# Hybrid conv, attention and mixture-of-experts kernel: the first batches rebuilt, with constants in order of need, weights over two queues, expert weights split later and the slot fill in pieces

## What is computed

```python
# conv mixer
xn = (x - mean) / sqrt(var + 1e-5) * ln_w + ln_b          # over channels
bcdt = conv3x3(einsum('bchw,oc->bohw', xn, w_bcdt), w_gw, groups=32)
BC, dt = split(bcdt, 2)
AB = softmax(dt + A, over positions) * BC
y = einsum('bcs,bsn->bcn', einsum('bcn,bsn->bcs', x, AB), BC)
x = einsum('bchw,oc->bohw', y, w_out) + x
# attention over the 1024 tokens of a batch, u = _ln_t(t)
q, k, v = lrelu(u @ Wq + bq), lrelu(u @ Wk + bk), lrelu(u @ Wv + bv)
t = t + gamma * norm(softmax(mask(q @ k.T / 8)) @ v + u) + beta
# experts: one of 8 for each of 32768 tokens, capacity 5120 rows each
idx, prb = argmax and max of softmax(u2 @ gate_w + gate_b)
t = t + prb * (relu(u2 @ w1[idx] + b1[idx]) @ w2[idx] + b2[idx])   # where a row was free
```

## Time and profile before

| what | value |
|---|---|
| median of three runs | 2148.56 us (2146.14 to 2151.14) |
| the profiled execution | 2159.72 us |
| its span, first to last instruction | 2157.5 us |
| TensorE matmuls busy | 1991.0 us, 92% |
| VectorE busy | 1750.4 us, 81% |
| ScalarE busy | 1196.4 us, 55% |
| GpSimd busy | 1088.2 us, 50% |
| mean granted TensorE clock | 0.968 |

### The profile page before, as it was taken

The page is one execution under the profiler, slowest core; times in us unless marked ns, Lnnn a source line. Parts: engine busy times, 40 slices in busy tenths (PEclk is TensorE's granted clock), DMA queues, the critical chain, the costliest instruction groups (busy, mean ns, idle before and its releaser), DMA issues. The chain is left out here.

```text
span 2157.5 us, 41952 instructions
## 1 busy us (share of the span) xinstructions
PE 1991.0 (92%) x13855; PEld 1639.8 (76%) x13855; DVE 1750.4 (81%) x5467; ACT 1196.4 (55%) x2216; POOL 1088.2 (50%) x1243
## 2 busy tenths in 40 slices
PE   1669999999999999999999999999839999999996
PEld 1347787877878788787887878877629998888985
DVE  2257888888888888888888888888739998888985
ACT  0135555555555555555555555555427777777773
POOL 3111445555545545455454554544436665555554
PEclk9679999999999999999999999999959999999997
DMA  4911221221212212122121221212137777777874
GB/s 164 397 40 32 58 70 50 57 74 51 70 50 57 74 51 69 51 56 74 53 67 50 57 74 54 63 39 54 39 111 204 205 234 259 259 242 256 244 244 172
DMA packets 163511, 243.97 MB, mean 113 GB/s; under 512 B 31039, under 2 KB 110478, under 8 KB 163296
## 3 DMA queue, kind: packets, MB, share of 16 engines
q1 hardware_dynamic: 146016, 209.46, 32.2%
q0 software_dynamic: 17280, 31.84, 4.5%
HBM read 115.95 MB, written 95.56 MB: 98 GB/s over the span
## 5 line engine op out<-in xcount | busy, mean ns | idle before, releaser
L1184 PE MATMUL pvp<-va,pT 128*128 128x129 f32 x4096 | 503.3, 275 | 0.4 <-ACT pT L727 0.3
L1184 PEld LDWEIGHTS pvp<-va,pT 128*128 128x128 f32 x4096 | 484.1, 191 | 21.5 <-issue 11.1
L641 POOL DMA_INDIRECT expert_slots<-rows,slot_i x256 | 378.0, 1476 | 99.3 <-issue 89.8
L1355 POOL DMA_INDIRECT token_rows<-res x284 | 308.8, 1087 | 231.8 <-DVE res L1488 162.3
L727 ACT ACTIVATE pT<-stp 128x512 f32<-128x512 f32 x512 | 293.1, 596 | 132.9 <-PE stp L1158 126.9
L839 DVE TENSOR_REDUCE mxs<-mxp 128x1 f32<-128x512 f32 x512 | 336.0, 683 | 37.6 <-PE mxp L1061 27.3
L1541 PEld LDWEIGHTS e_yp<-w2s,hid 128*128 128x128 f32 x2272 | 294.2, 192 | 20.3 <-ACT hid L1418 0.3
L1541 PE MATMUL e_yp<-w2s,hid 128*128 128x128 f32 x2272 | 299.9, 275 | 0.0
L1418 ACT ACTIVATE hid<-e_hp,b1c 128x512 f32<-128x512 f32 x284 | 195.3, 688 | 113.8 <-PE e_hp L1533 105.5
L1061 PE MATMUL mxp<-khi,qhi 127*128 127x512 f32 x512 | 218.4, 469 | 13.7 <-issue 11.2
L1156 PE MATMUL stp<-qhl,klh 128*128 128x512 f32 x512 | 223.5, 436 | 3.1 <-DMA qhi<-nt 1.9
(11 more groups left out here) (242 smaller groups left out, 3836.6 us busy)
## 6 DMA issues: line engine op xcount, KB each, us to landing
w1p<-w_parts SPq DMA_DIRECT2D x71, 512.0 KB
expert_slots<-fill SPq DMA_DIRECT2D x32, 660.0 KB, 11.3
e_rows<-expert_slots SPq DMA_DIRECT2D x71, 264.0 KB, 4.9
w2s<-in_w SPq DMA_DIRECT2D x71, 256.0 KB
xs<-in_x SPq DMA_DIRECT2D x32, 512.0 KB, 4.8
token_rows<-rows SPq DMA_DIRECT2D x32, 512.0 KB, 3.8
f_rows<-token_rows SPq DMA_DIRECT2D x32, 512.0 KB, 6.9
out<-f_cols SPq DMA_DIRECT2D x32, 512.0 KB, 7.5
```

The lines of the kernel that those rows point to most:

```text
L641: g.indirect_dma_start(out=slots, out_offset=bass.IndirectOffsetOnAxis(ap=slot_i[k][:, t:t + 1], axis=0), in_=rows[k][:, t, :], in_offset= ...
L1184: last = mm(pvp[qt % 2][:, 0:VA], pT[c][:, kt, n * P:(n + 1) * P], va[k][:, kt, :], start=(kt == 0), stop=(kt == NT - 1))
L1355: g.indirect_dma_start(out=tokens, out_offset=bass.IndirectOffsetOnAxis(ap=res[n % 2][:, q, TOKEN:TOKEN + 1].bitcast(I32), axis=0), in_=re ...
```

## The change

The steps of a batch and their arithmetic stay. What changes:

- SP: x of batch 0, six loads on the new semaphore `w_first` (tap weights, w_bcdt_t, ln_w, w_bcdt_t again, ln_b, gate weights), x of batch 1, then w1 of experts 0 and 1. No further prologue.
- ScalarE's own queue: the other twelve loads (bq and bk on `bq_loaded`, ten on `w_loaded`).
- GpSimd: ident, mean_m (`ident_ready`); gmask, wtap, gwc, qkscale, img, neghalf (`early_ready`); pairs, the filler (`fill_ready`); the state selector after the root of batch 0's x statistics (`state_ready`); then all other constants (`mask_ready`).
- TensorE and VectorE: wln and the three small products come first and go to `mxp[0]`; the tap transposes (to `pvp`) come behind x_turn of batch 0, the tap copies behind its statistics. Waits for weights and constants stand at the first step that uses them.
- w1 of expert e is split on VectorE in step xs of batch 4 + e; SP stores it and loads w1 of expert e + 2 in step x_turn of batch 5 + e.
- The slot fill is issued from ScalarE's queue, two stores at a time, ahead of the steps bT_turn, dt, cd_turn, u1_turn, qk and qk_high until all 32 are out.
- `head`, `steps` and `tail` are written anew (484 steps in the head).

```diff
+FILL_STEP = 2
+W1_FIRST = 4
-        NW = 18
+        NW, NFIRST = 10, 6
@@ steps, one round of the loop
-        steps = [("t1b", 0), ("g", 2), (("mx", 0, 7), 1), (("st", 1, 7), 0), (("negmax", 0), 1), ("y", 2),
-                 (("mrow", 0), 1), ("ts", 2), (("pv", 1, 0), 0), ("u2_turn", -1), ("ln3s", -1), (("pv", 1, 1), 0),
-                 ("x_turn", 3), (("st", 0, 0), 1), ("xs", 3), (("u1n", 0), 2), (("u1n", 1), 2), (("pv", 1, 2), 0),
-                 ("gate", -1), (("pv", 1, 3), 0), (("u1n", 2), 2), (("st", 0, 1), 1), (("mx", 1, 0), 1),
...
+        steps = [(("mrow", 1), 0), ("t1b", 0), ("mask", 1), ("conv", 2), ("qk_high", 1), ("qk_low", 1),
+                 (("ln2n", 3), -1), ("dt", 2), ("dt_exp", 2), (("st", 1, 0), 0), (("st", 1, 1), 0), ("ln2m", -1),
...
+                 (("st", 1, 7), 0), ("y", 2), (("pv", 1, 0), 0), (("mrow", 0), 1), ("ts", 2), ("u2_turn", -1),
+                 (("pv", 1, 1), 0), ("gate", -1), ("ln3s", -1), (("pv", 1, 2), 0), (("u1n", 0), 2), (("u1n", 1), 2),
+                 (("u1n", 2), 2), (("mx", 1, 0), 1), (("pv", 1, 3), 0), (("st", 0, 0), 1), (("u1n", 3), 2),
+                 ("gate_turn", -1), (("st", 0, 1), 1), ("x_turn", 3), (("mx", 1, 1), 1), (("mx", 1, 2), 1),
...
@@ head, behind ts of batch 0
-                (0, "cd_turn"), (0, "h"), (0, "hh"), (0, "g"), (0, "y"), (0, "ts"), (0, ("u1n", 0)), (0, "mask"),
-                (0, ("u1n", 1)), (0, ("u1n", 2)), (0, ("u1n", 3)), (1, "x_turn"), (0, "u1_turn"), (1, "xs"),
-                (0, "qk"), (0, "v"), (1, "bcdt"), (1, "bT_turn"), (0, "t1b"), (0, "qk_lrelu"), (1, "conv"), (1, "dt"),
...
+                (0, "cd_turn"), (0, "h"), (0, "hh"), (0, "g"), (0, "y"), (0, "ts"), (1, "x_turn"), (0, ("u1n", 0)),
+                (0, ("u1n", 1)), (0, "mask"), (0, ("u1n", 2)), (0, ("u1n", 3)), (0, "u1_turn"), (1, "xs"), (0, "qk"),
+                (0, "qk_lrelu"), (0, "qk_high"), (0, "v"), (1, "bcdt"), (0, ("mx", 0, 0)), (0, ("mx", 0, 1)),
+                (0, "t1b"), (1, "bT_turn"), (0, ("mx", 0, 2)), (0, ("mx", 0, 3)), (0, "qk_low"), (0, ("mx", 0, 4)),
+                (1, "conv"), (1, "dt"), (1, "dt_exp"), (0, ("mx", 0, 5)), (0, ("mx", 0, 6)), (0, ("mx", 0, 7)),
+                (0, ("negmax", 0)), (0, ("mrow", 0)), (1, "cd_turn"), (0, ("mx", 1, 0)), (1, "h"), (0, ("st", 0, 0)),
...
@@ sync
-            w(wbc[:, 0, :], w_bcdt_t)
...
-            for e in range(E):
...
-            for f in range(NFILL):
...
+            sp.dma_start(gw_s[:], gate_w).then_inc(s["w_first"], 16)
             load_x(1, 1)
...
+            load_w1(0)
+            load_w1(1)
...
+                if st == "x_turn" and W1_FIRST < b <= W1_FIRST + E:
+                    e = b - W1_FIRST - 1
+                    wait_apart(sp, s["w1_parts"], e * 2 + 2, passed["sp"])
+                    sp.dma_start(w1parts[e], w1h[e % 2][:]).then_inc(w1_stored[e % 2], 16)
+                    if e + 2 < E:
+                        load_w1(e + 2)
@@ gpsimd
+            g.memset(neghalf[:], -0.5).then_inc(s["early_ready"], 1)
...
+                    if first:
+                        state_constants()
+                        pool.wait_ge(s["state_ready"], 1)
+                        late_constants()
@@ scalar
-            act.wait_ge(s["w_loaded"], 16 * NW)
-            act.wait_ge(s["mask_ready"], 1)
...
+            def fill_slots():
+                if filled[0] == 0:
+                    act.wait_ge(s["fill_ready"], 1)
...
+                for f in range(filled[0], min(filled[0] + FILL_STEP, NFILL)):
+                    act.dma_start(slots[f * P * FILL_ROWS:(f + 1) * P * FILL_ROWS].rearrange("(p r) d -> p (r d)", p=P),
+                                  fill[:].rearrange("p r d -> p (r d)")).then_inc(s["fill_done"], 16)
+                    filled[0] += 1
...
+                if st in ("bT_turn", "dt", "cd_turn", "u1_turn", "qk", "qk_high") and filled[0] < NFILL:
+                    fill_slots()
@@ vector
+                    if first:
+                        taps()
+                    if W1_FIRST <= b < W1_FIRST + E:
+                        w1_part(b - W1_FIRST)
@@ tensor
+            pe.wait_ge(s["w_first"], 16 * NFIRST)
+            pe.wait_ge(s["ident_ready"], 1)
             pe.wait_ge(s["wln_ready"], 1)
-            pe.wait_ge(s["taps_ready"], 1)
-            mm(work[:, 1, 256:256 + U], mean_m[:], wln[:], start=True, stop=True)
+            mm(mxp[0][:, 0:U], mean_m[:], wln[:], start=True, stop=True)
```

More of the change, by code:

```diff
@@ L530, in chain @@
                 pool.wait_ge(s["const_pool"], cp[0])
-            chain(g.memset(fill[:], 0.0))
-            g.memset(fill[:, :, TOKEN:TOKEN + 1].bitcast(I32), NO_TOKEN).then_inc(s["fill_ready"], 1)
             chain(g.memset(ident[:], 0.0))
@@ L536, in _ @@
                                   base=0, channel_multiplier=1))
-            chain(g.memset(ones_bf[:], 1.0))
-            chain(g.affine_select(out=before_bf[:], in_=ones_bf[:], pattern=[[1, P]], compare_op=ALU.is_gt, fill=0.0,
-                                  base=0, channel_multiplier=-1))
-            chain(g.tensor_copy(ident_bf[:], ident[:]))
-            chain(g.memset(mean_m[:], 1.0 / C))
-            chain(g.memset(pairs[:], 0.0))
-            for d in (U - S, U, U + S):
-                chain(g.affine_select(out=pairs[:], in_=pairs[:], pattern=[[-1, U]], compare_op=ALU.not_equal, fill=1.0,
-                                      base=-d, channel_multiplier=1))
-            chain(g.memset(wtap[:], 0.0))
-            chain(g.memset(ident2[:], 0.0))
-            for d in range(2):
-                for j in range(Q4):
-                    own = ident2[:, d * S:(d + 1) * S]
-                    chain(g.affine_select(out=own, in_=own, pattern=[[-1, S]], compare_op=ALU.not_equal, fill=1.0,
-                                          base=-j * S, channel_multiplier=1))
+            g.memset(mean_m[:], 1.0 / C).then_inc(s["ident_ready"], 1)
             gm = gmask[:].rearrange("o (g i) -> o g i", i=2)
@@ L583, in _ @@
             chain(g.memset(img[:], 0.0))
-            for k in range(2):
-                chain(g.memset(qhi[k][U:P, :].bitcast(F32), 0.0))
-                chain(g.memset(qhi[k][U:U + 1, :].bitcast(F32), 1.0))
-                chain(g.memset(khi[k][U:P, :].bitcast(F32), 1.0))
-                chain(g.memset(va[k][:, :, C:VA], 1.0))
-            g.memset(neghalf[:], -0.5).then_inc(s["mask_ready"], 1)
+            g.memset(neghalf[:], -0.5).then_inc(s["early_ready"], 1)
+            pool.wait_ge(s["early_ready"], 1)
@@ new lines, in _, with state_constants @@
+            chain(g.memset(pairs[:], 0.0))
+            for d in (U - S, U, U + S):
+                chain(g.affine_select(out=pairs[:], in_=pairs[:], pattern=[[-1, U]], compare_op=ALU.not_equal, fill=1.0,
+                                      base=-d, channel_multiplier=1))
+            chain(g.memset(fill[:], 0.0))
+            g.memset(fill[:, :, TOKEN:TOKEN + 1].bitcast(I32), NO_TOKEN).then_inc(s["fill_ready"], 1)
+            def state_constants():
+                chain(g.memset(ident2[:], 0.0))
+                for d in range(2):
+                    for j in range(Q4):
+                        own = ident2[:, d * S:(d + 1) * S]
+                        ins = g.affine_select(out=own, in_=own, pattern=[[-1, S]], compare_op=ALU.not_equal, fill=1.0,
+                                              base=-j * S, channel_multiplier=1)
+                        if (d, j) == (1, Q4 - 1):
+                            ins.then_inc(s["state_ready"], 1)
+                        else:
+                            chain(ins)
@@ L860, in one @@
                 if st == "dt":
+                    if first:
+                        dve.wait_ge(s["w_loaded"], 16 * NW)
                     dve.wait_ge(s["conv_done"], b + 1)
@@ L1092, in one @@
                 if st == "conv":
+                    if first:
+                        pe.wait_ge(s["taps_ready"], 1)
                     pe.wait_ge(s["img_ready"], b + 1)
@@ L1099, in one @@
                 if st == "cd_turn":
+                    if first:
+                        pe.wait_ge(s["state_ready"], 1)
                     wait_apart(pe, s["cd_exp"], b + 1, passed["pe"])
@@ L1116, in one @@
                 if st == "g":
+                    if first:
+                        pe.wait_ge(s["w_loaded"], 16 * NW)
                     pe.wait_ge(s["h_ready"], b + 1)
@@ L1136, in one @@
                 if st == "mask":
+                    if first:
+                        pe.wait_ge(s["mask_ready"], 1)
                     pe.wait_ge(s["kflag_ready"], b + 1)
```

190 lines of the change are left out of this document (102 added, 88 removed), and 332 rows, old and new, of tables (head, steps, tail).

## The result

| | before | after |
|---|---|---|
| median of 20 runs each | 2151.31 us | 2142.63 us (2139.3 to 2149.46) |
| ratio, 95% interval | | 0.9958 (0.9948 to 0.9968) |
| profiled execution, its span | 2159.72, 2157.5 us | 2142.42, 2140.7 us |
| TensorE busy | 1991.0 us | 2003.1 us |

Faster, by 0.42% or about 9 us (the 2148.56 us in the table of the kernel before is the median of three of these runs); I had forecast 47 and a range that ended at 2121.

A forecast was written before the change was run, and what follows sets the result against it. TensorE bounds the middle; the start is a chain through all engines. Head 52, less 1 for expert weights, 3 for the loop and 1 for the drain, gives 47 us: 2148.56 to 2101 us, range 2087 to 2121.

The forecast's parts named there:

- Constants, weights, taps: Start of the kernel: constants by need, two weight queues, taps apart; batch 0's statistics at 12.9 us, not 49.25: 36.3 us.
- New order of the head: Head up to batch 2's convolution: that starts at 109 us instead of 161.7, gain 52 us including the 36.3.
- Fill in pieces: Slot-fill stores on ScalarE's queue until batch 2: cost 0.3 us twice on the path, bounds 0 and 40 us.
- Rival 1: Head, batches 0 to 2: fill transfers delay q,k parts and score rows, giving back 20 us: 2121; chance 0.20.
- Expert weights in batches 4 to 11: Eight weight splits moved into these batches cost VectorE between 0 and 9 us; taken as 1.
- New order of the loop: Repeated steps: costs 0.1 us a batch, 3 us over 27 batches, between -4 and +14.
- Rival 3: Loop: TensorE stalls at gate behind u2's copy and at second-half maxima, 2 us a batch, 54 us: 2155; chance 0.05.
- The drain: End of the token part: eight score tiles stand together at ScalarE's pace, costing 1 us.
- rival 2: Head: TensorE's clock is full throughout, 9 us less, 1 already counted: 2093; chance 0.13.
- The test I had set: Batch 2's image at 108 us with a gain under 40 us blames the loop; its period says by how much.

The follow-up runs named there:

- prologue alone: Changed kernel with the head, steps and tail lists of the kernel before; constants, weights, split and fill as changed: 2124.15 us, 0.988 of the kernel before.
- order alone: Kernel before with only the three new lists (head, steps, tail): 2178.64 us, 1.0147 of the kernel before.
- fill in batch 0: Changed kernel with five fill stores a step instead of two during batch 0: 2139.29 us, 0.9948 of the kernel before.
- the new head and the old loop and drain: Changed kernel with the new head order cut to 513 steps, loop and tail of the kernel before: 2115.10 us, 0.9836 of the kernel before.
- gamma early: Changed kernel with loop steps ln2m and ln2g moved right behind the last ln2n, ahead of dt: 2207.96 us, 1.0271 of the kernel before.
- second try: Changed kernel with u2_turn and gate one pv later, second half's first maxima behind the second score tile: 2222.35 us, 1.032 of the kernel before.
- scatter right behind pos: Changed kernel with the loop's scatter step moved right behind pos, instead of behind the last maxima: 2255.71 us, 1.0497 of the kernel before.
- third try: Changed kernel with u2_turn and gate one pv later, second half's first maxima right behind the first score tile: 2138.95 us, 0.9944 of the kernel before.

## Why the prediction was wrong

**Constants, weights, taps: right.** First statistics 12.15 us (12.9 worked out), t1 38.29 (39.2), u1 44.37 (45.3). The gate weights were issued at 3.95 us and landed 2.8 us later, at 6.8, ahead of my 8.0. The prologue alone passed the 36.3 us on in full (36.6 at batch 1, 37.9 at batch 2) and then lost 7.1 between batches 2 and 3, in the same place as the changed kernel. Its fill pieces travel beside q,k parts there as well; no run took them away, so for that run the cause is argued.

**New order of the head: right to batch 2.** Maxima at 62.83 (64), conv of batch 1 at 66.51 (68.2), t1 at 84.53 (86.5), conv of batch 2 at 110.28 (109): 51.4 us against 52. Where I went wrong is that I ended the account at that convolution. 52 us was the lead there, and I took the lead there for the gain. The sum 52 - 1 - 3 - 1 = 47 has no term for the stretch from batch 2 to 3; as measured it is 51.5 - 12.4 - 24.5 - 4.5 = 10.1, with the expert weights inside the 24.5.

**Fill in pieces: the step that failed in the head.** I had 0.3 us twice and looked at what the stores cost ScalarE. Their price fell on SP's queue: a mask row behind q,k parts, 5.6 us of TensorE, with VectorE's queue behind it. Of the 12.4 us by batch 3, 8 go when that wait goes or falls to 1.6 us (46.9 and 47.0 us from batch 2 to 3 instead of 54.9). Some 4 stay, also in the order alone, which has no pieces on ScalarE's queue (46.5, against 42.5 before); what they are is open. Part of the 12.4 is the clock: TensorE's busy time in the stretch is 47.70 us at 0.91 here, 43.89 at 1.00 with the fill in batch 0 (42.46 before). Rival 1 named the mechanism, with 20 us for what cost 8. Its argument against fails twice. The pairs are not 5 us apart (109.69 and 111.25 us belong to two). And a small row needs more than an engine's time: 2.19 us of issue and 8.3 us until its reader starts, while the engines' share is 1.00.

**Rule and row.** The DMA share of 1.00 from 110 to 120 us, with stores from one queue and q,k parts from another, is where the rule cited in the prediction (the Trainium skill, DMA: Bandwidth & Descriptors, "Issuing engines are not separate DMA queues") bears: transfers interleave on the same 16 engines whoever starts them. I used it for the weights, where it changed nothing, and not for the fill, where it spoke against a free move. The trace agrees with it there.

**Expert weights in batches 4 to 11: right.** The period is 45.89 us in batches 7 to 11 and 45.77 later, 0.12 us for each split, 1 us in all (I took 1).

**New order of the loop: the term that was mis-sized, and the sign of the surprise.** I took 0.1 us a batch with an upper end of 14 us; it was 0.89, 24.5 us to batch 31, beyond that end. The 0.1 had no row behind it; in its place stands the wait behind GpSimd, 0.53 us a batch, and 0.36 that stay open. "No row prices this" was wrong: the trace had the slack, though not in the rows I showed. Before, beta ended 3.4 us ahead of t1, and reading the wait ahead of L896 and what stands on GpSimd in front of it would have shown a chain one could check against the new lists. Rival 3 had the sign, the wrong place (gate and u2's copy) and a price twice too high; 24.5 us was not enough to turn the sign.

**The drain: mis-sized too.** I took 1 us. From the image of batch 31 to the expert part's first matmul it is 139.2 us before, 143.7 in the changed kernel, 139.6 in the prologue alone and 139.7 with the new head and the old loop and drain. The runs with the new last steps have 142.2 to 144.0, with two buffers for t1 or three. So the 3 to 4.5 us belong to the order; which of its waits they are is open.

**Clock.** From 100 to 150 us it rose from 0.62 to 0.90, so rival 2 was right in part. Conv of batch 1 took 5.34 us, as in the steady loop (8.45 before); this is inside the 51.4 us. Conv of batch 2 took 7.12, and at the late maxima, from 120 to 130 us, where TensorE is busy 6.98 of 10 us, the clock is 0.66; both are in the 12.4 us behind.

The test I had set: image of batch 2 near 108 and a gain under 40 us blames the loop, "and the period says by how much". Image 109.5, gain 9, period 45.77: it pointed right, but of the 41.4 us between 51.5 and 10.1, 12.4 lay ahead of batch 3.

## What to carry to other kernels

A head start at one point is not a gain until the next stage has taken it over: work it out to the first batch of the steady stage, queue by queue, those of the transfers too. A loop bound by one engine at 99.9% hides every slack of the others; before its order is changed, list for each buffer that is used again how long before its reader's turn the last user is done. If a stall moves on when the stalled step is moved, look at what its releaser waits for; here one more buffer gave back 0.53 of 0.89 us a batch, and the best of five moves of steps 0.23. And parts of a change should be timed apart: here the prologue with the new head was worth 34 us, and the new loop and drain took 26 of it back.

## What the runs showed of the hardware

- Issuing a DMA has no fixed price. Two fill stores behind each other on ScalarE's queue took 0.82 us together; with q,k parts from SP's queue in flight, single ones took 1.25 and 1.48 us, and SP's 4 KB row 2.19. Five in a row on ScalarE's queue took 5.88 us, with no q,k part beside them.
- No engine's busy share points at the cost of the new loop: VectorE is at 86%, GpSimd at 47%, and still a chain through GpSimd is what held TensorE.
- A wait of TensorE can cost more than itself. From 500 to 1000 us the granted clock was 1.00 before and in the changed kernel, but 0.97, 0.96 and 0.96 in gamma early, the second try and scatter right behind pos, whose waits were up to 2.8, 3.3 and 5.3 us long. TensorE's busy time a batch rose there from 44.84 to 45.8, 46.7 and 46.4 us.
- Entering score or maxima tiles from another kind of matmul takes 0.31 to 0.34 us to the next start in most cases instead of 0.24. Behind conv and qk it is 0.63 each in the new loop, 0.49 and 0.63 in the old. The new loop has 15 such entries a batch, the old one 14; the third try has 14 too and a period of 45.54, so their number does not explain the loop's cost.
